# PSUM banks of a 16-sequence transformer kernel: four score banks and three dense banks in place of five and two

## What is computed

```python
x = x + attn_a(layernorm(x))   # 16 heads of 16, window of +-32 tokens and 4 global tokens, softmax
x = x + ffn(layernorm(x))      # silu(x wg) * (x wu), hidden size 768, then wd
x = x + attn_b(layernorm(x))   # 16 heads of 16, causal; numerator from rotated q and k,
                               # denominator from q and k as they are, over all 512 keys
x = x + ffn(layernorm(x))
```

## Time and profile before

| | us |
|---|---|
| median of three runs | 2284.94 |
| lowest and highest | 2279.85, 2287.68 |
| the profiled execution, its own time | 2286.64 |
| its span, first to last instruction | 2284.9 |
| PE busy | 1942.2 (85%) |
| ACT busy | 1447.9 (63%) |
| DVE busy | 1400.6 (61%) |
| POOL busy | 785.3 (34%) |
| mean granted TensorE clock, of full speed | 0.929 |

### The profile page before, as it was taken

The page is one execution under the profiler, slowest core; times in us unless marked ns, Lnnn a source line. Parts: engine busy times, 40 slices in busy tenths (PEclk is TensorE's granted clock), DMA queues, the critical chain, the costliest instruction groups (busy, mean ns, idle before and its releaser), DMA issues.

```text
span 2284.9 us, 63345 instructions
## 1 busy us (share of the span) xinstructions
PE 1942.2 (85%) x25221; PEld 1397.1 (61%) x25221; DVE 1400.6 (61%) x2971; ACT 1447.9 (63%) x3580; POOL 785.3 (34%) x1131
## 2 busy tenths in 40 slices
PE   5677889899897989989898988989899898979785
PEld 4463657566675756667575666757566675756445
DVE  5363657576675757567575756757575675755533
ACT  1228676676767666676766667675666767667480
POOL 0023233334334333433433343343334334334331
PEclk7688989999999999999999999999999999999887
DMA  6214343342434334243433424343342434333221
GB/s 186 71 42 97 61 119 83 93 95 75 108 73 110 81 99 96 75 102 75 106 80 99 97 73 102 73 111 78 99 95 77 101 72 112 79 91 93 60 63 33
DMA packets 129637, 201.87 MB, mean 88 GB/s; under 512 B 26769, under 2 KB 60561, under 8 KB 129313
## 3 DMA queue, kind: packets, MB, share of 16 engines
q1 hardware_dynamic: 129344, 197.80, 36.3%
HBM read 67.87 MB, written 51.52 MB: 52 GB/s over the span
## 4 chain that ended last, share of the span: by engine, by line
PE 58%; ACT 14%; DVE 11%; DMA 7%; issue 4%; SPq 4%; POOL 1%; ACTq 0%; POOLq 0%; DVEq 0%
PE gu_bank L1051 15%; PE d_bank L1067 7%; PE gu_bank L1079 6%; PE gu_bank L1015 5%; ACT s_bank L1165 5%; DMA xn<-o_scr_B 4%; PE s_bank L982 4%; PE s_bank L946 4%; ACT probs_B L1155 3%; SPq L574 3%; PE gu_bank L1025 3%; PE s_bank L812 2%; PE s_bank L967 2%; DVE xn L1372 2%; DMA o_scr_B<-o_raw 2%
## 5 line engine op out<-in xcount | busy, mean ns | idle before, releaser
L1165 ACT ACTIVATE s_bank<-s_bank 128x512 f32<-128x512 f32 x1024 | 602.6, 591 | 191.6 <-PE s_bank L946 190.8
L1574 POOL TENSOR_TENSOR h<-tmp,h 128x512 fp32r<-128x512 f32 x192 | 252.0, 1312 | 458.7 <-DVE h L1455 458.7
L1155 ACT ACTIVATE probs_B<-s_bank 128x512 f32<-128x512 f32 x640 | 334.5, 609 | 46.0 <-PE s_bank L967 43.2
L1051 PE MATMUL gu_bank<-xT,w_g 128*128 128x256 f32 x1536 | 238.2, 300 | 25.6 <-DVE tmp L1438 23.4
L1051 PEld LDWEIGHTS gu_bank<-xT,w_g 128*128 128x128 f32 x1536 | 211.1, 201 | 52.8 <-DVE tmp L1438 37.2
L1051 PE MATMUL gu_bank<-xT,w_u 128*128 128x256 f32 x1536 | 240.3, 297 | 2.7 <-DVE tmp L1444 0.5
L1194 ACT ACTIVATE tmp<-gu_bank 128x512 f32<-128x512 f32 x192 | 114.4, 596 | 197.2 <-PE gu_bank L1051 189.6
L1051 PEld LDWEIGHTS gu_bank<-xT,w_u 128*128 128x128 f32 x1536 | 208.1, 198 | 35.7 <-issue 20.4
L1438 DVE SCALAR_TENSOR_TENSOR tmp<-tmp,gu_bank 128x512 f32<-128x512 f32 x192 | 130.9, 682 | 159.5 <-ACT tmp L1194 158.1
L1067 PE MATMUL d_bank<-w_d,h 128*128 128x256 f32 x1536 | 225.3, 289 | 3.3 <-POOL h L1574 3.3
L946 PE MATMUL s_bank<-pack_b 48*128 48x512 f16 x1024 | 184.6, 406 | 45.8 <-DMA pack_b<-src_b 30.9
(11 more groups left out here) (140 smaller groups left out, 3288.0 us busy)
## 6 DMA issues: line engine op xcount, KB each, us to landing
pack_b<-src_b SPq DMA_DIRECT2D x768, 64.0 KB, 2.4
pack_a<-src_a SPq DMA_DIRECT2D x384, 64.0 KB, 2.3
x<-in_L_attn_a_x_dram SPq DMA_DIRECT2D x32, 512.0 KB, 4.7
o_scr_A<-o_raw SPq DMA_DIRECT2D x64, 256.0 KB, 2.4
o_scr_B<-o_raw SPq DMA_DIRECT2D x64, 256.0 KB, 2.4
xn<-o_scr_A SPq DMA_DIRECT2D x32, 256.0 KB
rden_on<-r_scr_A SPq DMA_DIRECT2D x32, 256.0 KB
x_scr<-x SPq DMA_DIRECT2D x16, 512.0 KB, 2.8
```

The lines of the kernel that those rows point to most:

```text
L1051: last = pe.matmul(bank[:, f * D:(f + 1) * D], plain(w[:, k, c:c + P], exact), plain(given[:, k, half * D:(half + 1) * D], exact), start=k ...
L1155: act.activation(probs["B"][:, i, :], score_bank("NP", n // 2, q, n % 2)[:, :], ACT.Exp, scale=SM_SCALE)\
L1165: act.activation(bank[:, :], bank[:, :], ACT.Exp, scale=SM_SCALE, accum_out=den[:, 0, j, 2 * tile + e, t:t + 1]).then_inc(den_exp, 1)
L1574: pool.tensor_tensor(h[1][:, i % 2, :], tmp[:, i % 2, :], h[0][:, i % 2, :].bitcast(F32), ALU.subtract)\
```

## The change

The score ring gets four banks, the dense ring three; with `d_bank` it is eight banks as before. The tables of places, the list of steps, and so the order of every engine's work stay as they are. A score step now waits for the holders four banks back in the ring, in place of five; a dense step waits for the release of the use three before it, in place of two.

```diff
-BANKS = 5
+BANKS, DENSE_BANKS = 4, 3
...
-        gu_bank = [ctx.enter_context(nc.psum_tensor(f"gu_bank{i}", [P, S], F32)) for i in range(2)]
+        gu_bank = [ctx.enter_context(nc.psum_tensor(f"gu_bank{i}", [P, S], F32)) for i in range(DENSE_BANKS)]
...
         def gu_of(kind, n, block, q, k=0):
-            return gu_bank[gu_use(kind, n, block, q, k) % 2]
+            return gu_bank[gu_use(kind, n, block, q, k) % DENSE_BANKS]
...
                 use = gu_use(kind, n, block, q, k)
-                if use > 1:
-                    pe.wait_ge(gu_taken, use - 1)
-                return gu_bank[use % 2]
+                if use >= DENSE_BANKS:
+                    pe.wait_ge(gu_taken, use - DENSE_BANKS + 1)
+                return gu_bank[use % DENSE_BANKS]
```

## The result

Three runs of the changed kernel took 2342.22 to 2345.63 us, median 2344.55. The ratio to the kernel before is 1.0267, with a 95% interval of 1.0235 to 1.0298: slower by 60 us. The forecast was 2366 us, with a range of 2316 to 2435.

What follows compares the result with a forecast made beforehand. PE's time in its fixed order was taken as the bound. Score waits of 115 us less a dense gain of 34 made 81 us, added to 2286.6 us, less 1.7 to the median: 2366 us, range 2316 to 2435.

Steps and rivals of the forecast that it cites:

- The signs named ahead: Turn over 136 us, PE idle about 20 us a turn, L1438 and L1473 waits nearly gone, new waits at L1365.
- The score term: Five clusters of score steps waiting for the fourth bank back: 7.2 us per sequence, 115 us slower.
- A: Cluster at 1132 to 1137 us: numerator pair waits for the values' bank and delays the up projection; 1.6 us.
- B: Cluster at 1171 to 1176 us: maxima pair waits for the values' bank, numerator pairs follow late; 1.8 us.
- C: Cluster at 1180 to 1191 us: values step waits for an exponential, denominator pair for its copy; 1.8 us.
- D: Cluster around 1209 us: values of attention A, turning of denominators and two earlier pairs come late; 1.1 us.
- E: Cluster from 1238 us: four late steps, two covered by the wait for attention B's output; 0.9 us.
- 24 late steps: Score steps in one turn whose new holder is released over 0.1 us too late; lateness adds up to 12.3 us.
- The first rival: Every score-bank lateness is paid in full: 11.2 us per sequence, 2430 us; chance 0.16.
- The dense term: PE's waits at L1051, L1079 and L1087, 44.1 us; the third dense bank gains 34 after 10.0 given back.
- the third rival: PE's clock also falls in the stretches of clusters A and B: 67 us over the forecast, 2433 us; chance 0.09.
- The second rival: PE's idle 14.8 us a turn swallow the score waits while the dense gain stays: 2241 us; chance 0.04.

Runs made afterwards that it cites:

- the repairs: Four score and three dense banks, with one or more steps moved on PE, DVE or ACT to win back time; ratios 1.0234 to 1.0268.
- two and with four repairs: Four and three banks: two up projections moved ahead, 2340.04 us; with DVE's copy and ACT's exponentials also ahead, 2340.32 us.
- the same edit: Third down projection of second FFN ahead of last gate projection: ratio 0.9953 on five and two banks, 1.0365 on four and three.

## Why the prediction was right, and what was off

**What bounds.** PE's fixed order did. The change left the busy times of DVE, ACT and POOL within 1%, and 48 of 59 us are idle time of PE. Idle time is not the whole of it: in the run with four and two banks PE was idle for 86 us more than before and busy for 35 more, for the same work. The signs named ahead came: the turn is longer than 136 us, the waits at L1438 and L1473 are gone, and copies at L1365 hold L967, L812 and L946. PE's idle time per turn grew less than was said, to 18.3 and not to about 20.

**The score term** was 7.2 us a sequence, 115 us, and the run with four and two banks measured 122. By cluster: A 1.6 forecast and 1.5 measured, B 1.8 and 1.9, C 1.8 and 1.8, D 1.1 and 1.2. The last two are from the comparison of starts between the kernel before and the one with four and two banks; in C the values step came 0.63 later, the pair behind its copy 0.80, and the two pairs ahead 0.39 together. In E the forecast had let the wait for attention B's output cover two late steps, which saved 18 us of the run. That wait did shrink, by 19 us, here before and with four and two banks:

```profile
PE gu_bank L1015 <- DVE xT L1380: 63.0, 20, 12.1
```

```profile
PE gu_bank L1015 <- DVE xT L1380: 43.7, 21, 11.8
```

The walk compared starts with releases, so that lost overlap was in it without being named. In the 24 late steps, adding up each lateness gave 12.3 us, 197 us of the run; walking through with the delay carried on gave the right size. The first rival, with 179 us, is excluded by the same run.

But the reason given for A was half wrong. The step "Behind it in PE's order is the up projection ... It moves to 1137.2, and the pairs now at 1136.90 to 1138.5" named the up projection as what costs. With it out of the way nothing was won, as the pair after next waited for the exponentials instead. Both paths end at the same time.

**The dense term** is what failed: "I take 44.1 - 10.0 = 34 us, and the ends 0 and 44". It measured 62, outside its own ends. Two things were missing: waits for dense banks at L1431, L1467 and L1444, which make 44.1 into about 56, and what a wait costs beyond the idle time that its row shows. By the comparison of starts, four banks with two dense ones against three, the three places that the forecast counted gave 3.15 us a turn with 2.64 of idle time, and the others 1.56; 0.77 went back at the values step behind the swap. The rest, 3.9 us a turn, is 63 us in 16 turns. The sentence "That is about all that a third dense bank can give" took idle time for an upper end, which it is not. The 10 us given back at the swap were right: L982 waits 10.2 us for ACT at L1148, 0.7 us each time, a wait that PE does not have with four and two banks.

**The sum** came out 21 us too high, from 7 too little on the loss and 28 too little on the gain. The first error hid a part of the second, which was luck.

**The clock.** It is 0.96 over 13 turns before and after, so the third rival did not decide this change. By the rule of the Trainium skill ("TensorE: Matmul & The Clock Gate", section "A second HAM failure mode: psum-queue depth-cycling"), frequent short idles of PE between groups of matmuls make the clock swing. This case's traces do not show that here: a turn has 3.3 us more idle time, in short waits, and its clock is the same. Nor do the repairs settle it. PE's busy time was 1953.1 us after the change, 1959.1 and 1962.5 with two and with four repairs, but 1944.5 to 1951.4 with one, and 1976.8 with the most waits of all, at four and two banks.

**The other side.** The second rival fell: new waits in the full stretch were paid, and what was swallowed is the part that the forecast had counted so. Where a later wait for a DMA followed, in the run with the exponentials ahead, a gain was swallowed as that rival had it for losses.

## What to carry to other kernels

Before taking a buffer from a ring, list for each step when its new holder is released and carry the delay along; a plain sum of latenesses was 60% too high here. The gain of a buffer given elsewhere is more than the idle time that ends at its release, since a wait also costs the overlap of two steps; count all releasers, not the largest three, and where two traces have the same order, compare starts, as neither PE's rows of waits nor those of the weight loads give the delay. A move that fills one wait should be checked for the queue that its late step enters: the same edit gave 12 us with five score banks and cost 22 with four.

## What the runs showed of the hardware

A matmul group that does not wait began 0.07 or 0.16 us before the modelled end of the group ahead, so 0.16 us of idle time stood for 0.45 us of delay, and 0.69 for 0.96. And turns of the same kernel differ by their clock. Two turns of the changed kernel that follow each other, with the columns of the earlier trace rows:

```profile
1163.82:1298.16 134.34, 115.62 (x1575) 83.86 (x1574) 85.03 (x181) 89.97 (x223) 48.99 (x70) 0.99 0.37 89
1298.16:1440.28 142.12, 122.76 (x1575) 89.25 (x1574) 87.99 (x190) 91.24 (x227) 48.57 (x70) 0.93 0.37 86
```

The second took 7.8 us longer at nearly the same idle time (18.7 and 19.4). A gain of a few us a run can drown in this, and some of the experiments above stay open in size.
